# Mamba block and mixture of experts on one core: the state scan split into one-state scans, half of them with their decay in PSUM, and three rotating banks for h1 and h2

## The chip, the cores and the metric

The kernel runs on one core of a Trainium2 chip. The metric is device time in microseconds. The kernel before has a median of 1651.7 us over 3 runs (1649.79 to 1654.0).

## The reference

Input x is 32 sequences of 256 tokens with 128 features. Two layers follow, each with a residual. The first is a selective state-space block (inner width 256, 16 states); the second is a mixture of eight experts and a shared one, of which every token uses the top four by weight, all computed densely.

```python
# layer 1, on the layernorm of x
x_and_res = x @ W_in;  u, res = halves;  u = silu(u)
delta = softplus(u @ W_delta + b_delta);  Bm = u @ W_B;  Cm = u @ W_C;  A = -exp(A_log)
# for each token in order, h is (256, 16) per sequence
h = exp(delta[..., None] * A) * h + delta[..., None] * Bm[:, None, :] * u[..., None]
y_t = einsum('bdn,bn->bd', h, C_t)
x = x + ((y + u * D) * silu(res)) @ W_out
# layer 2, on the layernorm of the new x; H = 341
gate = x @ Wg.T + bias;  weights = softmax over the top 4 of 8
h1, h2 = x @ W1[e].T, x @ W2[e].T
out = shared(x) + sum_e weights[e] * ((sigmoid(h1) * h1 * h2) @ W3[e].T)
```

## The kernel before

The tokens are cut into 16 tiles of 512 (two sequences each). Every tile goes through a chain of steps, and each of the five engine programs has a written order of steps (SP_ORDER, PE_ORDER, ACT_ORDER, DVE_ORDER, POOL_ORDER). The order is one body of a software pipeline: the letter ahead of a step says which tile it works on (SHIFT: f is tile j+1, m is j, e is j-1, d is j-2, c is j-3, b is j-4). Bodies -1 to 5 are written out, 6 to 14 run in a hardware loop (Fori), 15 to 19 are written out again; a body at either end leaves out the parts whose tile doesn't exist.

The first layer of a tile. xT, wi, wi_res, dz, bt, ct are TensorE steps into the one `side` bank; ScalarE and VectorE read them (L466, L540, L541, L611). GpSimd makes `delta` and `du` (L428, L433). b_out and bbc on the SyncE queue write the B rows to memory and read them back spread over all partitions, two states (1024 elements) at a time. The 16 states are handled in 8 groups of two (GN), the 256 channels in two halves (NH), so there are 16 units (NU), `arg` = 2 x group + half. For each, GpSimd writes du x B of both states into a ring buffer `hb` (dbu, L440), ScalarE writes two exponentials into a ring of eight `decay` buffers (decay, L552), and VectorE runs one scan in place over both states, 1024 elements (scan, L617). Column 0 of each sequence of `decay` is a zero set once, which restarts the scan. TensorE then turns the states (turn.0 to 31, four 128x128 transposes each, L802) into two `turn` banks, where VectorE multiplies by C and adds up in `acc` (sum, L630); state 0 is done by ScalarE (first, L525). Then yT, z, ymul, wo and x1 end the layer.

The second layer of a tile. x1T, xh and xl split the normalized input into a high and a low part. There are 24 hidden tiles of 128: h12.k is six matmuls (L836 to L838) of which three fill an h1 bank and three an h2 bank, two banks of each. silu.k (L563) reads h1 on ScalarE, gated.k (L694) multiplies it by h2 on VectorE into a ring of eight, w3.k (36 steps, L847) multiplies by W3 into `eo_bank`, ev.0 to 8 (L701, L706) add the experts up. gate, gate_exp, gem, ginv and w compute the routing weights.

ScalarE needs one table for exponentials and another for silu; a switch in the order is a table load (L490).

PSUM has eight banks: two h1, two h2, one `eo_bank`, two `turn`, one `side`.

The waits that the change touches. h1 of tile k waits for silu k-2, and h2 of tile k for gated k-2:

```python
for banks, hi, lo, free, full in ((h1_bank, w1h, w1l, s_ready, h1_full),
                                  (h2_bank, w2h, w2l, gated_ready, h2_full)):
    wait_before(pe, free, turn, NK, arg - 1)
```

dbu waits until the transposes of the group that used its buffer are done (`turned_before`, from HB_RING), turn waits until both scans of its group are done.

Of the kernel before, what the change touches and what calls it, by code (L numbers as in the profile page):

```python
# [6 lines left out]
ALU = mybir.AluOpType  # L7
# [3 lines left out]
P = 128  # L11
SEQ = 256
# [4 lines left out]
NS = 16  # L17
# [36 lines left out]
HB_RING = 4  # L54
BB_RING = 4
GATED_RING = 8
S_RING = 3
GATE_STEPS = 12
ABSENT = -3.0e38
CHOSEN = 3.0e38  # L60
TABLE_OF = {"soft": "natural_log_exp_and_others", "decay": "natural_log_exp_and_others",
# [11 lines left out]
d:turn.11 c:w3.6.7 d:wi_res.1 d:turn.12 c:h12.10 d:turn.13.14 c:w3.8.9.10 e:xT.0 c:w3.11 c:h12.11.12 e:wi.0  # L73
d:turn.15 c:w3.12 c:h12.13 d:turn.16.17 e:wi.1 d:turn.18 c:w3.13.14 c:h12.14.15 d:turn.19 c:w3.15 e:bt.0
d:turn.20.21 c:h12.16.17 d:turn.22 e:dz.0 c:h12.18 d:turn.23 c:w3.16.17.18.19 d:turn.24 e:dz.1 c:h12.19.20
d:turn.25 c:w3.20.21 d:turn.26.27.28.29.30.31 c:w3.22 d:yT.0 c:w3.23 d:yT.1 c:h12.21 c:w3.24.25.26.27 c:h12.22
# [16 lines left out]
e:scan.5 d:gated.5.6 e:sum.7
# [20 lines left out]
def mamba_moe_kernel(nc, x, w_in, w_delta, b_delta, w_b, w_c, a_log, d_param, w_out, wg_t, bias, w1_all,  # L114
# [7 lines left out]
    SHIFT = {"f": 1, "m": 0, "e": -1, "d": -2, "c": -3, "b": -4}  # L122
# [25 lines left out]
    with ctx:  # L148
# [40 lines left out]
        decay = sb("decay", [P, DA_RING, GN, TOK])  # L189
# [34 lines left out]
        h1_bank = [bank(f"h1_{i}") for i in range(2)]  # L224
        h2_bank = [bank(f"h2_{i}") for i in range(2)]
# [5 lines left out]
        consts, blank = sem("consts"), sem("blank")  # L231
# [14 lines left out]
        dbu_ready, decay_ready, scanned = sem("dbu_ready"), sem("decay_ready"), sem("scanned")  # L246
# [138 lines left out]
        def _(pool):  # L385
# [8 lines left out]
            pool.memset(decay[:, :, :, :].rearrange("p r n (b t) -> p (r n b) t", t=SEQ)[:, :, 0:1], 0.0).then_inc(consts, 1)  # L394
# [67 lines left out]
        def _(act):  # L462
# [17 lines left out]
            def program(j, parts):  # L480
# [3 lines left out]
                for part, step, arg in steps["act"]:  # L484
# [18 lines left out]
                    elif step == "xh":  # L503

                        wait_before(act, h2_full, turn, NK, 0)
# [24 lines left out]
                    elif step == "bt":  # L530
                        wait_before(act, b_stored, turn, 16, 0)
                        wait_before(act, c_ready, turn, 1, 0)
                        read_side(j, parts, part, step, arg, cbT[:, :], side[0:2 * NS, :], ACT.Copy, cbT_ready)
                    elif step == "zb":

                        wait_before(act, delta_ready, turn, 1, 0)
                        wait_before(act, du_ready, turn, 1, 0)
                        wait_before(act, decay_ready, turn, NS * NH, 0)
                        act.wait_ge(side_full, side_index(j, parts, part, "dz", arg))
                        act.activation(soft[:, arg, :], side[:, :], ACT.Abs, bias=bd_sb[:, arg:arg + 1]).then_inc(soft_steps, 1)  # L540
                        act.activation(delta[:, arg, :], side[:, :], ACT.Relu, bias=bd_sb[:, arg:arg + 1]).then_inc(zb_ready, 1)  # L541
                    elif step == "soft":
                        act.wait_ge(soft_steps, count(turn, 4, 2))
                        act.activation(soft[:, :, :], soft[:, :, :], ACT.Exp, scale=-1.0).then_inc(soft_steps, 1)
                        act.wait_ge(soft_steps, count(turn, 4, 3))
                        act.activation(soft[:, :, :], soft[:, :, :], ACT.Ln, bias=one[:, :]).then_inc(soft_steps, 1)
                    elif step == "decay":
                        grp, h = divmod(arg, NH)
                        act.wait_ge(delta_ready, count(turn, 1, 1))
                        wait_before(act, scanned, turn, NU, arg - DA_RING + 1)  # L550
                        for i in range(GN):
                            act.activation(  # L552
                                decay[:, arg % DA_RING, i, :].rearrange("p (b t) -> p b t", t=SEQ)[:, :, 1:],
                                delta[:, h, :].rearrange("p (b t) -> p b t", t=SEQ)[:, :, 1:],
                                ACT.Exp, scale=a_sb[:, h, GN * grp + i:GN * grp + i + 1]).then_inc(decay_ready, 1)
                    elif step == "gate_exp":
                        act.wait_ge(gate_steps, count(turn, GATE_STEPS, GATE_STEPS))
                        wait_before(act, gem_ready, turn, 1, 0)
                        act.activation(gm[:, :, :], gm[:, :, :], ACT.Exp).then_inc(gex_ready, 1)
                    elif step == "silu":  # L560
                        act.wait_ge(h1_full, count(turn, NK, arg + 1))
                        wait_before(act, gated_ready, turn, NK, arg - S_RING + 1)
                        act.activation(s[:, arg % S_RING, :], h1_bank[arg % 2][:, :], ACT.Silu).then_inc(s_ready, 1)  # L563
                    if isinstance(j, int) and j + SHIFT[part] == 0 and (step, arg) in (("zb", 1), ("decay", 9)):
                        cut_hi(step == "decay")
# [9 lines left out]
            act.wait_ge(consts, CONSTS)  # L575
            act.wait_ge(a_ready, 1)
# [4 lines left out]
        def _(dve):  # L581
# [17 lines left out]
            def program(j, parts):  # L599
                for part, step, arg in steps["dve"]:  # L600
# [12 lines left out]
                    elif step == "scan":  # L613
                        dve.wait_ge(decay_ready, count(turn, NS * NH, GN * (arg + 1)))
# [73 lines left out]
                    elif step == "gated":  # L688
# [5 lines left out]
                        dve.tensor_tensor(gated[:, arg % GATED_RING, :], h2_bank[arg % 2][:, :],  # L694
# [13 lines left out]
                    if isinstance(j, int) and j + SHIFT[part] == 0 and (step, arg) in (("c", 0), ("scan", 9)):  # L708
                        cut_lo(step == "scan")

            dve.wait_ge(a_exped, 1)
# [6 lines left out]
        def _(pe):  # L718
# [26 lines left out]
            def program(j, parts):  # L745
                for part, step, arg in steps["pe"]:
# [43 lines left out]
                    elif step == "turn":  # L790
                        n, pair = divmod(arg, 2)
                        grp, i_n = divmod(n, GN)
                        pe.wait_ge(scanned, count(turn, NU, NH * (grp + 1)))
# [32 lines left out]
                    elif step == "h12":  # L826
# [5 lines left out]
                        for banks, hi, lo, free, full in ((h1_bank, w1h, w1l, s_ready, h1_full),  # L832
                                                          (h2_bank, w2h, w2l, gated_ready, h2_full)):
                            wait_before(pe, free, turn, NK, arg - 1)
                            dst = banks[arg % 2][:, :]
                            pe.matmul(dst, hi[:, cols], xh[:, :], start=True, stop=False)  # L836
                            pe.matmul(dst, hi[:, cols], xl[:, :], start=False, stop=False)  # L837
                            pe.matmul(dst, lo[:, cols], xh[:, :], start=False, stop=True).then_inc(full, 1)  # L838
# [63 lines left out]
```

## Time and profile before

| | before |
|---|---|
| median of 3 runs | 1651.7 us |
| the profiled execution | 1652.92 us |
| its span | 1650.2 us |
| mean granted TensorE clock | 0.969 of full speed |
| busy: TensorE, VectorE | 1482.1, 1478.1 us |
| busy: ScalarE, GpSimd | 1116.9, 953.1 us |

The span is the time between the first and the last instruction that the profiler recorded on the core. Busy time is the union of an engine's instructions. TensorE's is overstated, since matmuls overlap in the records: the distance between starts is nearer to what one costs. VectorE's instructions overlap as well, by 0.07 to 0.09 us each.

### The profile page before, as it was taken

To read this page: it belongs to the slowest core of one execution; us is meant where nothing else is said; L and a number is where in the kernel's file an instruction comes from. 1 tells how busy PE (TensorE), PEld (TensorE's weight loads), DVE (VectorE), ACT (ScalarE), POOL (GpSimd) and SP (SyncE) were. 2 spreads that over 40 slices of the span, in tenths; PEclk is the share of its full clock that TensorE was granted. 3 is DMA by queue.
4 is the path that set the end of the run, shared out by engine and by line. 5 is a ranking of instruction groups with operands and counts; after the bars stand their busy time and mean duration, and the time that the engine had idled before them with its cause. 6 is when DMAs were issued, how large, how long until landed. Compare 5 with 4: busy or idle time off the path is not lost. (4 is left out here: it accounts for less than half of the span.)

```text
span 1650.2 us, 29548 instructions
## 1 busy us (share of the span) xinstructions
PE 1482.1 (90%) x9216; PEld 1216.3 (74%) x9216; DVE 1478.1 (90%) x2755; ACT 1116.9 (68%) x1611; POOL 953.1 (58%) x477
## 2 busy tenths in 40 slices
PE   3254999999999999999999999999999999999898
PEld 0133878787887778787777878777787878878687
DVE  0797999999999999999999999999999998999943
ACT  3444787776778687676868757686876777776431
POOL 2766566575756566484656648465664747475310
PEclk9576999999999999999999999999999999999999
DMA  4211012121111112110111211012121110212000
GB/s 147 100 52 51 27 53 71 52 69 45 46 37 59 64 52 71 52 57 15 57 64 52 71 52 57 15 58 64 52 71 52 58 45 22 65 53 65 1 8 7
DMA packets 50451, 86.87 MB, mean 53 GB/s; under 512 B 4647, under 2 KB 32804, under 8 KB 50340
## 3 DMA queue, kind: packets, MB, share of 16 engines
q1 hardware_dynamic: 50340, 85.66, 15.9%
q8 instruction: 37, 0.61, 0.2%
q14 instruction: 74, 0.61, 0.1%
HBM read 80.93 MB, written 4.72 MB: 52 GB/s over the span
## 5 line engine op out<-in xcount | busy, mean ns | idle before, releaser
L440 POOL TENSOR_TENSOR hb<-du,bbc 128x1024 f32<-128x1024 f32 x256 | 721.9, 2834 | 432.4 <-PE turn L802 431.8
L617 DVE TENSOR_TENSOR_SCAN hb<-decay,hb 128x1024 f32<-128x1024 f32 x256 | 613.0, 2411 | 10.9 <-POOL hb L440 10.6
L847 PE MATMUL eo_bank<-w_sb,gated 128*128 128x128 f32 x3840 | 482.6, 276 | 2.2 <-DVE o L706 2.2
L847 PEld LDWEIGHTS eo_bank<-w_sb,gated 128*128 128x128 f32 x3840 | 459.8, 192 | 17.2 <-issue 10.3
L802 PE MATMUL turn<-ident,hb 128*128 128x128 f32 x2048 | 321.0, 285 | 112.9 <-DVE hb L617 55.2
L563 ACT ACTIVATE s<-h 128x512 f32<-128x512 f32 x384 | 224.5, 598 | 280.1 <-PE h L838 258.5
L630 DVE SCALAR_TENSOR_TENSOR acc<-turn,c_sb,acc 128x256 f32<-128x256 f32 x960 | 405.0, 475 | 8.9 <-PE turn L802 5.2
L802 PEld LDWEIGHTS turn<-ident,hb 128*128 128x128 f32 x2048 | 246.9, 146 | 218.8 <-issue 79.0
L552 ACT ACTIVATE decay<-delta,a_sb 128x510 f32<-128x510 f32 x512 | 325.5, 711 | 8.0 <-POOL delta L428 6.7
L490 ACT ACT_TABLE_LOAD x247 | 316.9, 1283 | 4.4
L694 DVE TENSOR_TENSOR gated<-h,s 128x512 f32<-128x512 f32 x384 | 258.3, 680 | 38.2 <-PE eo_bank L847 20.0
L836 PE MATMUL h<-xh,w1h 128*128 128x512 f32 x384 | 187.7, 489 | 2.0 <-DVE xl L649 2.0
L706 DVE SCALAR_TENSOR_TENSOR o<-eo_bank,w,o 128x128 f32<-128x128 f32 x512 | 143.1, 343 | 34.2 <-PE eo_bank L847 33.6
L836 PE MATMUL h<-xh,w2h 128*128 128x512 f32 x384 | 152.8, 398 | 0.0
L837 PE MATMUL h<-xl,w2h 128*128 128x512 f32 x384 | 152.4, 397 | 0.0
L838 PE MATMUL h<-xh,w1l 128*128 128x512 f32 x384 | 152.3, 397 | 0.0
L838 PE MATMUL h<-xh,w2l 128*128 128x512 f32 x384 | 151.9, 395 | 0.0
L837 PE MATMUL h<-xl,w1h 128*128 128x512 f32 x384 | 151.7, 395 | 0.0
L838 PEld LDWEIGHTS h<-xh,w2l 128*128 128x128 f32 x384 | 72.4, 189 | 18.0
L836 PEld LDWEIGHTS h<-xh,w2h 128*128 128x128 f32 x384 | 72.5, 189 | 17.3 <-DVE gated L694 0.3
L837 PEld LDWEIGHTS h<-xl,w2h 128*128 128x128 f32 x384 | 72.5, 189 | 17.3
L838 PEld LDWEIGHTS h<-xh,w1l 128*128 128x128 f32 x384 | 72.3, 188 | 17.4
(81 smaller groups left out, 1186.9 us busy)
## 6 DMA issues: line engine op xcount, KB each, us to landing
bbc<-b_rows SPq DMA_DIRECT2D x128, 512.0 KB, 4.8
x_in<-x_dram SPq DMA_DIRECT2D x16, 256.0 KB, 2.8
x_cur<-x_dram SPq DMA_DIRECT2D x16, 256.0 KB, 3.0
out_dram<-o SPq DMA_DIRECT2D x16, 256.0 KB, 2.4
gated<-w_all_dram SPq DMA_DIRECT2D x2, 1534.5 KB, 7.3
w_sb<-w_all_dram SPq DMA_DIRECT2D x5, 192.0 KB
b_rows<-cbT SPq DMA_DIRECT2D x16, 32.0 KB, 1.6
w_in_sb<-w_in_dram SPq DMA_DIRECT2D x1, 256.0 KB, 3.1
```

Of the source, the lines that this page charges most:

```text
L440: pool.tensor_tensor(hb[:, arg % HB_RING, :, :], du[:, h, :].unsqueeze(1).broadcast_to((P, GN, TOK)), bbc[:, r, :].rearrange("p (n t) -> p ...
L490: act.preload_act_table_set(table)
L552: act.activation(decay[:, arg % DA_RING, i, :].rearrange("p (b t) -> p b t", t=SEQ)[:, :, 1:], delta[:, h, :].rearrange("p (b t) -> p b t" ...
L563: act.activation(s[:, arg % S_RING, :], h1_bank[arg % 2][:, :], ACT.Silu).then_inc(s_ready, 1)
L617: dve.tensor_tensor_scan(states, decay[:, arg % DA_RING, :, :].rearrange("p n t -> p (n t)"), states, 0.0, ALU.mult, ALU.add).then_inc(sca ...
L630: dve.scalar_tensor_tensor(acc[:, blk, :], turn_bank[pair][:, i * DI:(i + 1) * DI], c_sb[:, blk, n:n + 1], acc[:, blk, :], ALU.mult, ALU.add)\
L694: dve.tensor_tensor(gated[:, arg % GATED_RING, :], h2_bank[arg % 2][:, :], s[:, arg % S_RING, :], ALU.mult).then_inc(gated_ready, 1)
L802: mm = pe.transpose(turn_bank[pair][:, (NH * i + h) * P:(NH * i + h + 1) * P], src[:, blk * P:(blk + 1) * P], ident[:, :])
L836: pe.matmul(dst, hi[:, cols], xh[:, :], start=True, stop=False)
L837: pe.matmul(dst, hi[:, cols], xl[:, :], start=False, stop=False)
L838: pe.matmul(dst, lo[:, cols], xh[:, :], start=False, stop=True).then_inc(full, 1)
L847: mm = pe.matmul(eo_bank[:, blk * P:(blk + 1) * P], gated[:, k % GATED_RING, blk * P:(blk + 1) * P], w3_sb[:, pair, :], start=(n == 0), st ...
```

## The change

- A scan of two states (1024) becomes two steps, scan0 and scan1, of one state (512) each; each has a semaphore of its own (`scanned[i]`), and turn waits only for the scans of its own state.
- The decay of the even state of a group (decay0) goes to one PSUM bank, `decay_bank`, which holds one decay. decay0 of unit k waits for scan0 of unit k-1. The odd state's decay1 stays in a ring of eight buffers in SBUF, each half the size.
- `hb` has 8 buffers instead of 4.
- h1 and h2 are steps of their own on TensorE. They take turns in three banks: h1.k fills bank 2k mod 3, h2.k bank 2k+1 mod 3. h1.k waits for gated k-2, h2.k for silu k-1.
- All five orders are new. The parts b and a do work now (a: tile j-5, the store), so the pipeline is one body longer and the hardware loop runs from body 7.

```diff
-HB_RING = 4
+HB_RING = 8
+H_RING = 3
@@
-c:load_cur.0 c:bbc.4.5.6.7 d:b_out.0 d:bbc.0.1.2.3 m:load_x.0 b:store.0
+c:bbc.4 b:load_cur.0 e:load_x.0 c:bbc.5.6.7 d:b_out.0 d:bbc.0.1.2.3 a:store.0
@@ PE_ORDER, its beginning and end
-c:w3.1 c:h12.6 c:w3.2 d:wi_res.0 c:w3.3 d:turn.8 c:h12.7 d:turn.9 c:h12.8 c:w3.4 d:turn.10 c:w3.5 c:h12.9
...
-d:wo.0 c:h12.23 e:turn.0 e:ct.0 c:w3.28 e:turn.1 c:w3.29.30.31 e:turn.2 d:x1T.0 c:w3.32.33.34.35 d:h12.0
-e:turn.3 d:h12.1 e:turn.4 d:h12.2 e:turn.5 d:h12.3 e:turn.6 d:h12.4 e:turn.7 d:gate.0 d:w3.0 d:h12.5
+c:wo.0 b:h2.7 b:h1.7 d:turn.4 b:h1.8 d:turn.5 b:w3.4.5 b:h2.8 b:w3.6 b:h2.9 b:w3.7 d:wi_res.0 b:h1.9.10 d:turn.6
...
+b:h2.21 b:h1.21.22 b:w3.24.25 e:dz.1 b:w3.26 d:turn.21.22 b:w3.27 b:h2.22.23 c:x1T.0 d:turn.23 b:h1.23
+b:w3.28.29 d:turn.24.25 b:w3.30 c:h1.0 d:turn.26 c:h2.0 b:w3.31 c:h1.1 d:turn.27 c:h2.1 d:turn.28 b:w3.32
+d:turn.29 b:w3.33 c:h2.2 c:h1.2 d:turn.30.31 c:h1.3 b:w3.34.35 d:yT.0 c:h2.3.4 c:h1.4 e:turn.0 d:yT.1 c:w3.0.1
+e:ct.0 c:w3.2 e:turn.1 c:w3.3 c:gate.0 c:h1.5 e:turn.2 c:h1.6 c:h2.5 e:turn.3 c:h2.6
@@ ACT_ORDER, all of the new one
+b:silu.16.17 d:decay0.10 d:decay1.12.13.14 d:decay0.11 e:wi.1 b:silu.18.19 d:decay0.12 b:silu.20 d:decay0.13
+e:bt.0 d:decay1.15 d:decay0.14.15 e:zb.0 b:silu.21.22 e:zb.1 e:soft.0 c:x1T.0 c:xh.0 b:silu.23 e:decay1.0
+c:silu.0.1 e:decay1.1 e:decay0.0 e:decay1.2.3 e:decay0.1 c:silu.2.3.4 e:decay0.2 m:xn.0 e:first.0 e:decay0.3
+e:first.1 c:silu.5.6 e:decay1.4.5.6 e:decay0.4 c:gate_exp.0 c:silu.7.8 e:decay0.5 e:decay1.7.8.9 e:decay0.6
+e:wi_res.0 c:silu.9.10 e:ud.0 e:wi_res.1 c:silu.11.12 e:ud.1 c:silu.13 e:decay0.7 e:decay1.10 e:decay0.8
+e:decay1.11 m:xT.0 e:decay0.9 c:silu.14.15 d:x1n.0 m:wi.0
@@ DVE_ORDER, all of the new one
+b:ev.1 d:sum.5.6 b:gated.9 d:scan0.6 b:gated.10 d:scan1.4 b:gated.11 d:scan1.5.6 d:sum.7.8 b:ev.2 b:gated.12
+d:scan0.7 d:sum.9.10 d:scan0.8 b:gated.13 d:sum.11 b:ev.3 d:sum.12 b:gated.14.15 d:scan0.9 d:scan1.7 b:gated.16
+d:scan1.8.9 d:scan0.10 d:sum.13.14 b:gated.17 d:scan0.11 d:sum.15 b:gated.18 b:ev.4 d:sum.16.17 d:scan0.12
+b:gated.19 d:scan1.10 b:gated.20 d:scan0.13 d:sum.18 b:ev.5 d:scan0.14 d:scan1.11 d:sum.19 d:scan1.12 d:sum.20
+d:scan1.13.14 b:gated.21 d:sum.21 b:ev.6 d:scan1.15 d:sum.22.23 c:xl.0 b:gated.22 d:sum.24.25 b:gated.23
+d:scan0.15 d:sum.26 b:ev.7 d:sum.27 c:gated.0 d:sum.28.29 e:scan0.0 c:gated.1 d:sum.30.31 e:scan0.1 c:gated.2
+d:z.0 b:ev.8 c:gated.3 e:scan1.0 d:z.1 e:scan1.1 e:c.0 e:scan0.2 c:gated.4 c:ev.0 c:gate.0 e:sum.2 e:scan0.3
+c:gated.5 e:scan1.2 c:gated.6 e:sum.3 f:ln.0 e:scan0.4 d:x1.0 c:gated.7 e:scan1.3 c:ginv.0 e:scan0.5 e:sum.4
+c:gated.8
@@ POOL_ORDER
-c:dbu.15 d:delta.0 d:du.0 d:dbu.0.1 c:ymul.0 d:dbu.2 c:rstd1.0 d:dbu.3.4 m:rstd.0 d:dbu.5.6 c:gem.0 d:dbu.7
-c:w.0 d:dbu.8.9.10.11.12.13.14
+b:w.0 d:dbu.7.8.9.10 c:rstd1.0 d:dbu.11.12.13.14.15 m:rstd.0 e:delta.0 e:du.0 e:dbu.0.1.2.3 d:ymul.0 e:dbu.4.5
+c:gem.0 e:dbu.6
@@ banks
-        h1_bank = [bank(f"h1_{i}") for i in range(2)]
-        h2_bank = [bank(f"h2_{i}") for i in range(2)]
+        h_bank = [bank(f"h_{i}") for i in range(H_RING)]
+        decay_bank = bank("decay_bank")
@@ ScalarE
-                    elif step == "decay":
+                    elif step in ("decay0", "decay1"):
+                        i = int(step[-1])
...
-                        wait_before(act, scanned, turn, NU, arg - DA_RING + 1)
-                        for i in range(GN):
+                        wait_before(act, scanned[i], turn, NU, arg if i == 0 else arg - DA_RING + 1)
+                        dst = decay_bank[:, :] if i == 0 else decay[:, arg % DA_RING, :]
@@ VectorE
-                        states = hb[:, arg % HB_RING, :, :].rearrange("p n t -> p (n t)")
-                        dve.tensor_tensor_scan(states,
-                                               decay[:, arg % DA_RING, :, :].rearrange("p n t -> p (n t)"),
-                                               states, 0.0, ALU.mult, ALU.add).then_inc(scanned, 1)
+                        states = hb[:, arg % HB_RING, i, :]
+                        dve.tensor_tensor_scan(states, decay_bank[:, :] if i == 0 else decay[:, arg % DA_RING, :],
+                                               states, 0.0, ALU.mult, ALU.add).then_inc(scanned[i], 1)
@@ TensorE
-                        pe.wait_ge(scanned, count(turn, NU, NH * (grp + 1)))
+                        pe.wait_ge(scanned[i_n], count(turn, NU, NH * (grp + 1)))
...
+                        if step == "h1":
+                            wait_before(pe, gated_ready, turn, NK, arg - 1)
+                            hi, lo, fill, full = w1h, w1l, 2 * arg, h1_full
+                        else:
+                            wait_before(pe, s_ready, turn, NK, arg)
+                            hi, lo, fill, full = w2h, w2l, 2 * arg + 1, h2_full
+                        dst = h_bank[fill % H_RING][:, :]
```

## Rows read from the trace of the kernel before

**Rows 1.** The page, part 1: busy us, share of span, instructions of each engine.

```profile
PE 1482.1 (90%) x9216; PEld 1216.3 (74%) x9216; DVE 1478.1 (90%) x2755; ACT 1116.9 (68%) x1611; POOL 953.1 (58%) x477
```

**Rows 2.** Busy time of each engine in stretches: start:end, length, PE, PEld, DVE, ACT, POOL.

```profile
69.32:139.34 70.02, 35.10 (x136) 22.88 (x136) 65.72 (x76) 33.19 (x44) 51.13 (x19) 0.73 0.15 54
...
274.12:367.30 93.18, 90.50 (x578) 74.92 (x577) 89.63 (x173) 69.94 (x102) 57.94 (x30) 1.00 0.18 55
1509.49:1596.53 87.04, 78.79 (x512) 68.10 (x511) 71.64 (x147) 39.96 (x59) 28.18 (x15) 0.98 0.03 10
1596.53:1650.20 53.67, 48.38 (x318) 42.94 (x316) 21.14 (x52) 11.56 (x19) 0.49 (x2) 1.00 0.02 6
```

**Rows 3.** TensorE in order of time: start, length, line, shapes, count.

```profile
806.03 0.48 PE L836 MATMUL h<-xh,w1h 128*128 128x512 f32 x1
...
807.51 2.84 PE L847 MATMUL eo_bank<-w_sb,gated 128*128 128x128 f32 x24
810.11 0.48 PE L836 MATMUL h<-xh,w1h 128*128 128x512 f32 x1
```

**Rows 4.** VectorE's waits (total, times, longest): two from 274.12:367.3, two from 842.89:938.9.

```profile
DVE gated L694 <- PE eo_bank L847: 1.1, 1, 1.1
DVE xl L649 <- ACT xh L508: 0.9, 1, 0.9
...
DVE gated L694 <- PE eo_bank L847: 1.6, 2, 0.9
...
DVE o L701 <- issue: 0.7, 1, 0.7
```

**Rows 5.** SyncE's register instructions of the looped output store: durations, first and last start.

```profile
L378 SPq FUSED_REGOPS  x9: 57/57/57, 447.8 to 1214.3; - x9
```

**Rows 6.** VectorE, GpSimd and ScalarE in order of time, one looped body.

```profile
831.87 0.69 DVE L694 TENSOR_TENSOR gated<-h,s 128x512 f32<-128x512 f32 x1
832.46 0.87 DVE L630 SCALAR_TENSOR_TENSOR acc<-turn,c_sb,acc 128x256 f32<-128x256 f32 x2
833.25 2.29 DVE L617 TENSOR_TENSOR_SCAN hb<-decay,hb 128x1024 f32<-128x1024 f32 x1
...
845.82 5.01 ACT L552 ACTIVATE decay<-delta,a_sb 128x510 f32<-128x510 f32 x8
...
848.64 7.00 POOL L440 TENSOR_TENSOR hb<-du,bbc 128x1024 f32<-128x1024 f32 x2 [4.35 <-PE turn L802]
...
849.83 3.63 DVE L617 TENSOR_TENSOR_SCAN hb<-decay,hb 128x1024 f32<-128x1024 f32 x1
...
853.96 1.11 DVE L706 SCALAR_TENSOR_TENSOR o<-eo_bank,w,o 128x128 f32<-128x128 f32 x4
...
880.61 4.46 DVE L617 TENSOR_TENSOR_SCAN hb<-decay,hb 128x1024 f32<-128x1024 f32 x2
```

**Rows 7.** One line's instructions over the run: ns min/median/max, first and last start.

```profile
L617 DVE TENSOR_TENSOR_SCAN hb<-decay,hb x256: 2258/2281/4437, 45.9 to 1554.6; 128x1024 f32<-128x1024 f32 x128
...
L694 DVE TENSOR_TENSOR gated<-h,s x384: 657/681/695, 164.7 to 1638.5; 128x512 f32<-128x512 f32 x192
```

**Rows 8.** The scans' busy time in an unrolled body and in a looped one.

```profile
274.12:367.30 93.18, 36.70 (x16) 1.00 0.18 55
...
733.20:829.30 96.10, 38.02 (x16) 1.00 0.16 53
```

**Rows 9.** The page's groups: busy, mean ns of one | idle before, releaser.

```profile
L440 POOL TENSOR_TENSOR hb<-du,bbc 128x1024 f32<-128x1024 f32 x256 | 721.9, 2834 | 432.4 <-PE turn L802 431.8
...
L490 ACT ACT_TABLE_LOAD x247 | 316.9, 1283 | 4.4
```

**Rows 10.** VectorE in order of time: at tile 0's `xl`, and after the last `acc`.

```profile
160.99 0.69 DVE L649 TENSOR_TENSOR xl<-side,xh 128x512 fp32r<-128x512 f32 x1 [4.35 <-ACT xh L508]
...
1564.31 0.68 DVE L694 TENSOR_TENSOR gated<-h,s 128x512 f32<-128x512 f32 x1
```

**Rows 11.** The page, part 6: a DMA group, KB each, us to landing.

```profile
bbc<-b_rows SPq DMA_DIRECT2D x128, 512.0 KB, 4.8
```

More of the change, by code:

```diff
@@ L60 @@
 CHOSEN = 3.0e38
-TABLE_OF = {"soft": "natural_log_exp_and_others", "decay": "natural_log_exp_and_others",
+TABLE_OF = {"soft": "natural_log_exp_and_others", "decay0": "natural_log_exp_and_others",
+            "decay1": "natural_log_exp_and_others",
             "gate_exp": "natural_log_exp_and_others", "wi": "silu_and_others", "wi_res": "silu_and_others",
@@ L188, in mamba_moe_kernel @@
         bbc = sb("bbc", [P, BB_RING, GN * TOK])
-        decay = sb("decay", [P, DA_RING, GN, TOK])
+        decay = sb("decay", [P, DA_RING, TOK])
         hb = sb("hb", [P, HB_RING, GN, TOK])
@@ L245, in mamba_moe_kernel @@
         bbc_in = [sem(f"bbc_in_{r}") for r in range(BB_RING)]
-        dbu_ready, decay_ready, scanned = sem("dbu_ready"), sem("decay_ready"), sem("scanned")
+        dbu_ready = sem("dbu_ready")
+        decay_ready = [sem(f"decay_ready_{i}") for i in range(GN)]
+        scanned = [sem(f"scanned_{i}") for i in range(GN)]
         turned, summed = sem("turned"), sem("summed")
@@ L503, in program @@
                     elif step == "xh":
+                        wait_before(act, h1_full, turn, NK, 0)
                         wait_before(act, h2_full, turn, NK, 0)
@@ L537, in program @@
                         wait_before(act, du_ready, turn, 1, 0)
-                        wait_before(act, decay_ready, turn, NS * NH, 0)
+                        for i in range(GN):
+                            wait_before(act, decay_ready[i], turn, NU, 0)
                         act.wait_ge(side_full, side_index(j, parts, part, "dz", arg))
@@ L562, in program @@
                         wait_before(act, gated_ready, turn, NK, arg - S_RING + 1)
-                        act.activation(s[:, arg % S_RING, :], h1_bank[arg % 2][:, :], ACT.Silu).then_inc(s_ready, 1)
-                    if isinstance(j, int) and j + SHIFT[part] == 0 and (step, arg) in (("zb", 1), ("decay", 9)):
-                        cut_hi(step == "decay")
+                        act.activation(s[:, arg % S_RING, :], h_bank[2 * arg % H_RING][:, :], ACT.Silu).then_inc(s_ready, 1)
+                    if isinstance(j, int) and j + SHIFT[part] == 0 and (step, arg) in (("zb", 1), ("decay1", 9)):
+                        cut_hi(step == "decay1")
             def cut_hi(second):
@@ L575, in _ @@
             act.wait_ge(consts, CONSTS)
+            act.wait_ge(bank_blank, 1)
             act.wait_ge(a_ready, 1)
@@ L707, in program @@
                                                          ALU.mult, ALU.add).then_inc(ev_done, 1)
-                    if isinstance(j, int) and j + SHIFT[part] == 0 and (step, arg) in (("c", 0), ("scan", 9)):
-                        cut_lo(step == "scan")
+                    if isinstance(j, int) and j + SHIFT[part] == 0 and (step, arg) in (("c", 0), ("scan1", 9)):
+                        cut_lo(step == "scan1")
+            dve.memset(decay_bank[:, :].rearrange("p (b t) -> p b t", t=SEQ)[:, :, 0:1], 0.0).then_inc(bank_blank, 1)
+            dve.wait_ge(bank_blank, 1)
             dve.wait_ge(a_exped, 1)
@@ L825, in program @@
                         mm.then_inc(side_full, 1)
-                    elif step == "h12":
+                    elif step in ("h1", "h2"):
                         cols = slice(arg * P, (arg + 1) * P)
@@ L831, in program @@
                                 pe.wait_ge(w_lo, 2)
[L832 to L838, printed above, removed]
+                        if step == "h1":
[5 more added lines that the diff above has]
+                        dst = h_bank[fill % H_RING][:, :]
+                        pe.matmul(dst, hi[:, cols], xh[:, :], start=True, stop=False)
+                        pe.matmul(dst, hi[:, cols], xl[:, :], start=False, stop=False)
+                        pe.matmul(dst, lo[:, cols], xh[:, :], start=False, stop=True).then_inc(full, 1)
                     elif step == "w3":
```

39 lines of the change are left out of this document (14 added, 25 removed).

## The prediction

> **What bounds the kernel now.** I read the page's busy shares first: TensorE and VectorE both show 90% of the span, ScalarE 68%, GpSimd 58% [rows 1]. Two engines at 90% leave open which one sets the pace, so the next view is the busy time by stretch, cut at the start of each body of the program (the first `o<-eo_bank` of a tile on VectorE marks it). An unrolled body lasts 93.18 us and VectorE is busy 89.63 of it; TensorE's 90.50 overstates its load, since matmul records overlap [rows 2]. By their starts, the six matmuls of one hidden tile take 1.48 us (806.03 to 807.51) and 24 of the `eo_bank` ones 2.60 (807.51 to 810.11), 0.108 each [rows 3]. So a tile's MoE costs TensorE 24 x 1.48 = 35.5 and 240 x 0.108 = 26.0, its 128 transposes at the same 0.108 another 14; with about 13 for projections and side work, an estimate, that is some 88. VectorE is the bound, full but for 3.5 us of a body, of which the view of waits names 1.1 for `eo_bank` and 0.9 for `xh` [rows 4].
>
> Bodies inside the hardware loop are longer. The output stores of the nine looped bodies run from 447.8 to 1214.3: 766.5 / 8 = 95.8 us [rows 5]. The same stretch of orders in the loop shows where 2.6 us go: VectorE restarts late (0.7, "issue"), `gated` waits 0.5 more for TensorE, and one scan takes 3.63 us instead of 2.28 [rows 4, 6]. That last is a collision: two `hb` products on GpSimd began at 848.64, the scan at 849.83; the scan waited 1.35 us for the first product and the second product for the scan, so the two took 7.00 us [rows 6]. While one engine runs, the other waits. `gated`, with one operand in PSUM, never stretches: at most 695 ns over a median of 681, against 4437 over 2281 for a scan [rows 7].
>
> **The change, part by part.**
> *Scans.* 256 scans of 1024 become 512 of 512. A scan of 1024 costs 2.19 us when another follows (two in 4.46, one in 2.28 [rows 6, 7]). If an element takes two cycles of 0.96 GHz (1024 x 2 = 2133 ns), 57 ns are fixed; no row has a scan of another size, so this is an estimate. The nearest rows bound it: `gated`, PSUM and SBUF in, starts its successor after 0.60 us, 0.067 above 512/0.96; `acc`, 256 from PSUM, two in 0.79, costs 0.39, which leaves 0.125 [rows 6]. Lowest is no added cost, highest 0.125 in each new scan: +0 to +3 us a tile over 35.0. I take 0.057, the operation's own remainder: +0.9.
> *Half the decays in PSUM.* The port conflict goes for 16 of 32 scans. What is there to win is small: the 16 scans of an unrolled body take 36.70 against 16 x 2.281 = 36.50, so 0.2 us; in a looped one 38.02, so 1.5 [rows 7, 8]. GpSimd gets back some of what it waits (its product's mean is 2.83 us), but it idles 432 us before these products [rows 9] and is not late. Gain 0.1 us unrolled, 0.6 looped. The bounds are 0 and the full 0.2 and 1.5.
> *ScalarE.* The 32 exponentials stay (0.62 us each in a row, 8 in 5.01 [rows 6]). The order has 20 switches between the exponential and the silu table instead of 16, at 1283 ns: +5.1 us on an engine busy 69.94 of 93.18 [rows 2, 9]. Hidden in sum, but the bank for `decay0` holds one decay, so ScalarE and VectorE now alternate. The tightest stretch by my reading is decay0.10 to decay0.13: after decay0.10 ScalarE does 5 more exponentials up to decay0.12 (three decay1, two decay0), wi.1, silu.18 and 19, silu.20, decay0.13 and four table loads, 6 x 0.62 + 4 x 0.6 + 4 x 1.28 = 11.2 us. VectorE in the same stretch has three scan0 and one scan1 (4 x 1.12), sum.13 to 17 (5 x 0.78), gated.17 to 20 (4 x 0.6) and ev.4 (four `o` steps, 1.11 in a row, 1.04 without the overlap with the next [rows 6]): 11.8 us. It fits with 0.6 to spare, so I charge nothing; the cost if it does not fit is a rival.
> *Three banks.* h2(k) now waits for silu(k-1) and h1(k) for gated(k-2), where both had two banks of their own. TensorE loses one hidden tile half of running ahead (0.70 us) in each of ScalarE's exponential blocks, and has w3 and turn steps between. Bound 0 to 8 x 0.7 = 5.6 of its 6 us of slack; I take 0 for the period. Twice as many `hb` buffers (8) take away much of what GpSimd waits for; of VectorE's 3.5 idle I let 0.8 go.
> So an unrolled body is 89.7 + 0.9 - 0.1 + 2.7 = 93.2, no shorter than now; the loop's excess falls from 2.6 to 2.0.
> *Queues.* In SP's order load_cur and load_x, which wait for x1 and xn, now stand ahead of bbc.5 to 7, where they stood before bbc.4 and behind bbc.3; on GpSimd delta and du stand behind dbu.15, ymul behind dbu.3 of the next tile. A `bbc` transfer lands in 4.8 us [rows 11], GpSimd has over 30 us idle in a body of 93.18 (58 busy) [rows 2], and 8 `hb` buffers let products run ahead. I charge nothing; if a late x1 holds bbc.5 up, the scans behind it stand still for the same time, at most 4.8 a body.
> *The pipeline.* This is the part that moves the end. In the old order h12.0 of a tile stands beside turn.3 of the next; in the new one h1.0 stands behind turn.26 of the next, and parts b and a are new stages. The MoE of a tile is 23 of 32 transposes later. Steady bodies do not care; filling and draining do.
> Fill: VectorE went to tile 0's MoE up to 161.0 with a wait of 4.35 for `xh` [rows 10], and shorter ones before it. In the new order tile 1 reaches sum.4 without these and without tile 0's first `gated`, at about 158, an estimate. The next body (tile 1's scans, tile 2's start, the first seven hidden tiles of tile 0) lacks 15 `gated` and 32 `o` steps, 15 x 0.6 + 8 x 1.04 = 17.3: 90.5 - 17.3 + some 6.8 idle (tile 0 alone had 4.3 idle in 70.0 [rows 2]) = 80. Full bodies begin at 238.
> Full bodies 4 to 16: 13 x 93.2 + 8 looped x 2.0 = 1227.6.
> Body 17 (last scans, no new tile): the old one took 87.04 with 78.8 TensorE busy [rows 2]; the new one has less side work, 84.
> Drain: after the last `acc` at 1564.3 the old kernel needed 85.9 us [rows 10]. The old last body (18 hidden tiles, 35 w3 steps of 6.7 matmuls or 0.72 us) is 18 x 1.48 + 35 x 0.72 = 51.8 by rows and took 53.67 [rows 2, 3], so 1.9 over. The new one has body 18: 17 hidden tiles and 32 w3 steps of tile 14, then wo, x1T and gate (28 matmuls, 3.1), seven hidden tiles and four w3 steps of tile 15: 24 x 1.48 + 36 x 0.72 + 3.1 = 64.5; and body 19 with 17 x 1.48 + 32 x 0.72 = 48.2. With 1.9 over each, 116.
> Span 238 + 1227.6 + 84 + 116 = 1665.6. The same sum for the old kernel is 180.8 + 14 x 94.9 + 87.0 + 53.7 = 1650.2 (the first is what is left: body 17 begins at 1509.5, and 14 bodies lie before it). The profiled execution took 1652.92 with that span, 2.7 more, and lies 1.2 above the median of 1651.7. So 1665.6 + 2.7 - 1.2 = **1667**.
>
> In other words: filling and draining cost 18 us more, the shorter loop excess gives 5 back, the rest about 3.
>
> **Rivals.** *VectorE's idle goes.* The finer steps and 8 `hb` buffers might close the gaps: a body of 91.5 (90.5 busy, 1.0 idle) and only the loop's 0.65 restart: 438 + 13 x 91.5 + 8 x 0.65 = 1633 span, 1634. For it: nearly all of today's idle is four named waits. Against: VectorE's load itself does not fall. The point from which this kernel beats the old one is a body of 92.0.
> *Handshake through one bank.* ScalarE reaches decay0 late, and scan0 waits, at the four tight places of a body, 0.5 us each (half a silu or a late TensorE step): +2 x 14 = 28, 1695. For: a spare of 0.6 us in 11.8, one wait on PE in it breaks it. Against: the other decay0 have 0.7 us or more. It decides from 0.6 us of delay per lap.
> *PSUM read at full fixed price.* scan0 pays 0.125 as `acc` does, not 0.057: 16 x 0.068 = 1.1 a body, +15, 1682. For: `acc` reads PSUM. Against: so does `gated`, with 0.067. The Trainium skill, "VectorE: DVE Perf Modes", section on the TRN2 errata, gives 120 fixed cycles from PSUM against 58 from SBUF; an estimate by it is 62 cycles, 65 ns, for each scan0, the same 15 us. No row here shows a scan reading PSUM.
> *No change in sum.* Body at 92.0 to 92.3, 1650 to 1655.
> *The change doesn't free the port.* Then the looped collision stays: +0.6 x 8 = 5, inside the range. [...]
>
> **Numbers.** Forecast or near it (1657 to 1676) 0.35; fixed price 0.13; handshake 0.12; VectorE's idle goes 0.27; no change 0.13. A measurement tells 0.3%, 5 us, from none. Faster than 1646.7: 0.28; within 5 us of 1651.7: 0.13; slower: 0.59. The range leaves a tenth at each end: 1632 to 1694; that of the forecast alone is 1657 to 1676.
>
> **What would show it.** Scan groups with a mean near 1.21 us, scan0 with a maximum near its median and scan1 not; 32 of them 36 us of a body. VectorE's unrolled bodies near 93, looped ones near 95. The first `gated` of tile 0 near 210 instead of 164.7, and after the last `acc` some 125 us instead of 86. ScalarE with about 20 table loads a body and no scan0 waiting for it. It would be wrong if bodies fell below 92, if scan0 waits for ScalarE, if `gated` or h waits on each other's banks for over 1 us a body, or if the drain takes under 110 us.

## The result and the profile after

The changed kernel takes 1610.4 us (median of 4 runs, 1608.65 to 1611.48), the kernel before 1652.85 in the same comparison (4 runs): a ratio of 0.974, 95% interval 0.972 to 0.976. It is 42 us faster; 15 slower had been forecast, with 1632 as the low end of the range. The profiled execution took 1608.65 with a span of 1606.9.

The stretches of VectorE's bodies, as in [rows 2]: an unrolled body (start:end, length, then busy PE, PEld, DVE, ACT, POOL), a looped one, and the drain from the last `acc` on.

```profile
308.09:397.94 89.85, 88.93 (x578) 74.77 (x578) 89.47 (x190) 74.93 (x106) 49.69 (x30) 1.00 0.16 57
761.19:852.85 91.66, 89.33 (x578) 74.78 (x578) 89.87 (x189) 74.93 (x106) 49.78 (x30) 1.00 0.16 55
1478.90:1606.90 128.00, 122.69 (x799) 108.68 (x797) 58.42 (x165) 34.53 (x57) 4.91 (x9) 1.00 0.03 9
```

The unrolled body fell from 93.18 to 89.85 us, and VectorE is busy 89.47 of it, where it was 89.63 of 93.18 [rows 2]. It has nearly the same work; its idle time went from 3.55 to 0.38 us. The looped body fell from 96.0 to 91.7 us, and there both parts shrank: busy time from 91.42 to 89.87, idle time from 4.6 to 1.8. The old kernel's looped body:

```profile
842.89:938.90 96.01, 91.38 (x573) 75.59 (x572) 91.42 (x172) 69.26 (x100) 58.42 (x30) 0.98 0.17 53
```

The page's groups after (busy, mean ns of one | idle before, releaser), against [rows 7, 9]:

```profile
L450 POOL TENSOR_TENSOR hb<-du,bbc 128x1024 f32<-128x1024 f32 x256 | 617.6, 2436 | 217.0 <-PE turn L817 212.7
...
L631 DVE TENSOR_TENSOR_SCAN hb<-decay_bank,hb 128x512 f32<-128x512 f32 x256 | 310.2, 1212 | 13.3 <-POOL hb L450 12.0
L631 DVE TENSOR_TENSOR_SCAN hb<-decay,hb 128x512 f32<-128x512 f32 x256 | 316.2, 1252 | 0.0
```

GpSimd's product costs 2436 ns instead of 2834: it hardly waits for scans. Over the run (ns min/median/max) the scans with the PSUM decay never stretch, those with two SBUF operands do, at most to 3297:

```profile
L631 DVE TENSOR_TENSOR_SCAN hb<-decay_bank,hb x256: 1190/1210/1225, 45.6 to 1470.2; 128x512 f32<-128x512 f32 x128
L631 DVE TENSOR_TENSOR_SCAN hb<-decay,hb x256: 1190/1210/3297, 49.1 to 1464.1; 128x512 f32<-128x512 f32 x128
```

VectorE has two waits in the looped body (total, times, longest); for the unrolled body the same view names none:

```profile
DVE o L719 <- issue: 1.1, 1, 1.1
DVE acc L643 <- PE turn L817: 0.2, 1, 0.2
```

The waits of [rows 4] for `eo_bank` and `xh` are gone from both bodies. "issue" is VectorE's restart after the loop's branch.

A scan with both operands in SBUF and a product of GpSimd exclude each other [rows 6]; what they contend for is called the port here. How the new orders keep clear of it shows in one stretch of a looped body, in order of time. The product pair at 795.12 runs under `acc`, `gated` and other work, the scan at 799.17 is a PSUM one, and SBUF scans follow only once the pair is done, at 799.86.

```profile
795.12 4.74 POOL L450 TENSOR_TENSOR hb<-du,bbc 128x1024 f32<-128x1024 f32 x2 [0.92 <-PE turn L817]
...
799.17 1.21 DVE L631 TENSOR_TENSOR_SCAN hb<-decay_bank,hb 128x512 f32<-128x512 f32 x1
800.30 1.20 DVE L631 TENSOR_TENSOR_SCAN hb<-decay,hb 128x512 f32<-128x512 f32 x1
```

The run split by the forecast's own terms, in us. Body 4, body 17 and the drain begin at 234.25, 1414.48 and 1497.94, each marked by the first `o<-eo_bank,w,o` of a tile:

| | forecast | measured |
|---|---|---|
| until body 4 | 238 | 234.3 |
| bodies 4 to 16 | 1227.6 | 1180.2 (90.8 each) |
| body 17 | 84 | 83.5 |
| drain | 116 | 109.0 |
| span | 1665.6 | 1606.9 |

### The profile page after: what moved, and what is told of

It reads as the page before. It is cut to its first block, busy times and chain, and to the rows that moved or that the text cites. A ratio compares the mean times of both kernels' runs of the same rounds, so it can differ in the third digit from the quotient of the medians.

```text
span 1606.9 us, 30312 instructions
## 1 busy us (share of the span) xinstructions
PE 1470.4 (92%) x9216; PEld 1215.4 (76%) x9216; DVE 1461.6 (91%) x3012; ACT 1176.7 (73%) x1659; POOL 805.8 (50%) x477
## 4 chain that ended last, share of the span: by engine, by line
PE 64%; DVE 13%; issue 10%; ACT 9%; POOL 3%; DMA 1%; DVEq 1%; SPq 0%; ACTq 0%; POOLq 0%
PE eo_bank L865 20%; PE turn L817 9%; PE h L854 9%; PE h L855 8%; PE h L856 8%; DVE hb L631 6%; PE side L787 3%; PE side L781 3%; DVE acc L643 2%; ACT L500 2%; PE side L794 2%; POOL hb L450 2%; DVE gated L707 2%; ACT decay L565 1%; DVE o L719 1%
## 5 line engine op out<-in xcount | busy, mean ns | idle before, releaser
L450 POOL TENSOR_TENSOR hb<-du,bbc 128x1024 f32<-128x1024 f32 x256 | 617.6, 2436 | 217.0 <-PE turn L817 212.7
L865 PEld LDWEIGHTS eo_bank<-w_sb,gated 128*128 128x128 f32 x3840 | 472.2, 192 | 40.2 <-issue 18.0
L865 PE MATMUL eo_bank<-w_sb,gated 128*128 128x128 f32 x3840 | 495.5, 276 | 7.2 <-DVE o L719 7.2
L631 DVE TENSOR_TENSOR_SCAN hb<-decay_bank,hb 128x512 f32<-128x512 f32 x256 | 310.2, 1212 | 13.3 <-POOL hb L450 12.0
L631 DVE TENSOR_TENSOR_SCAN hb<-decay,hb 128x512 f32<-128x512 f32 x256 | 316.2, 1252 | 0.0
L565 ACT ACTIVATE decay_bank<-delta,a_sb 128x510 f32<-128x510 f32 x256 | 175.6, 686 | 153.2 <-DVE hb L631 152.0
L707 DVE TENSOR_TENSOR gated<-h,s 128x512 f32<-128x512 f32 x384 | 257.5, 674 | 30.6 <-PE h L856 14.1
L854 PE MATMUL h<-xh,w2h 128*128 128x512 f32 x384 | 180.7, 471 | 0.7 <-ACT s L575 0.7
L565 ACT ACTIVATE decay<-delta,a_sb 128x510 f32<-128x510 f32 x256 | 170.6, 708 | 7.0 <-POOL delta L438 6.5
L438 POOL TENSOR_TENSOR delta<-delta,soft 128x1024 f32<-128x1024 f32 x16 | 37.9, 2368 | 231.6 <-ACT soft L558 231.6
L456 POOL TENSOR_TENSOR y<-y,sres 128x1024 f32<-128x1024 f32 x16 | 50.5, 3159 | 108.9 <-DVE y L649 108.9
```

What stands on the lines that cost most here:

```text
L450: pool.tensor_tensor(hb[:, arg % HB_RING, :, :], du[:, h, :].unsqueeze(1).broadcast_to((P, GN, TOK)), bbc[:, r, :].rearrange("p (n t) -> p ...
L565: act.activation(dst.rearrange("p (b t) -> p b t", t=SEQ)[:, :, 1:], delta[:, h, :].rearrange("p (b t) -> p b t", t=SEQ)[:, :, 1:], ACT.Ex ...
L631: dve.tensor_tensor_scan(states, decay_bank[:, :] if i == 0 else decay[:, arg % DA_RING, :], states, 0.0, ALU.mult, ALU.add).then_inc(scan ...
L707: dve.tensor_tensor(gated[:, arg % GATED_RING, :], h_bank[(2 * arg + 1) % H_RING][:, :], s[:, arg % S_RING, :], ALU.mult).then_inc(gated_r ...
L865: mm = pe.matmul(eo_bank[:, blk * P:(blk + 1) * P], gated[:, k % GATED_RING, blk * P:(blk + 1) * P], w3_sb[:, pair, :], start=(n == 0), st ...
```

## The experiments

Each was timed in 4 runs beside the kernel before; the medians of that kernel were 1651.8 (e1 to e4), 1653.0 (e5 to e8) and 1652.2 (e9 to e11).

### e1: decay0 in SBUF

```diff
-        decay_bank = bank("decay_bank")
+        decay_bank = sb("decay_bank", [P, TOK], mybir.dt.bfloat16)
```

> The changed kernel with decay0's one buffer in SBUF instead of PSUM (as bf16, since SBUF has no room for 2 KB; so the decays of the even states are rounded). The orders, the three banks and the eight hb buffers stay. Theory P (the port): the changed kernel lost VectorE's idle because 16 of 32 scans of a tile no longer take the second SBUF port. Then scan0 collides again with the hb products of GpSimd: its maximum goes from 1225 ns to over 2000, the products' mean from 2436 to 2700 or more, and a body grows by 2 to 4 us, 1640 to 1665. Theory S (slack): the idle went because the new orders and eight hb buffers let every engine run ahead, and the port is worth only what scans were seen to lose before (0.2 us an unrolled body, 1.5 a looped one). Then collisions come back but a body grows by under 1 us, 1611 to 1625.

1746.9 us, ratio 1.058 (1.056 to 1.060), 136 above the changed kernel. The scans and products of this kernel:

```profile
L450 POOL TENSOR_TENSOR hb<-du,bbc 128x1024 f32<-128x1024 f32 x256 | 687.0, 2705 | 229.5 <-PE turn L817 222.9
L631 DVE TENSOR_TENSOR_SCAN hb<-decay_bank,hb 128x512 f32<-128x512 bf16 x256 | 443.3, 1732 | 13.3 <-POOL hb L450 12.2
```

```profile
L631 DVE TENSOR_TENSOR_SCAN hb<-decay_bank,hb x256: 1191/1226/3422, 47.8 to 1605.1; 128x512 f32<-128x512 bf16 x128
```

The minimum is that of the PSUM scans (1190), so neither the type nor the place makes a scan longer by itself; the mean went from 1212 to 1732. 443.3 - 310.2 = 133 us more in scan0 and 6 in scan1 make up the whole difference of the spans (1741.8 - 1606.9 = 135). An unrolled body of this kernel:

```profile
259.63:357.50 97.87, 90.40 (x576) 74.81 (x576) 97.51 (x189) 75.34 (x106) 56.28 (x30) 1.00 0.16 52
```

VectorE is busy 97.51 of 97.87 us: it idles 0.36, no more than in the changed kernel (0.38), and is busy 8.1 us longer. So theory P is right that the port decides, at 136 us instead of the 30 to 55 it gave, but wrong on the idle time. VectorE's waits are gone with the port conflict back as well; what the PSUM decay saves in these orders is stretched scans.

### e2: the old kernel with split scans

```diff
-                        states = hb[:, arg % HB_RING, :, :].rearrange("p n t -> p (n t)")
-                        dve.tensor_tensor_scan(states,
-                                               decay[:, arg % DA_RING, :, :].rearrange("p n t -> p (n t)"),
-                                               states, 0.0, ALU.mult, ALU.add).then_inc(scanned, 1)
+                        for i in range(GN):
+                            states = hb[:, arg % HB_RING, i, :]
+                            scan = dve.tensor_tensor_scan(states, decay[:, arg % DA_RING, i, :], states, 0.0,
+                                                          ALU.mult, ALU.add)
+                        scan.then_inc(scanned, 1)
```

> The kernel before with each scan of 1024 as two scans of 512, back to back, all in SBUF, nothing else changed. By the prediction a split adds 57 ns: 16 x 0.057 = 0.9 us a body, +14 over 15 bodies, 1666. The rival: the changed kernel's body shows VectorE busy 89.47 us where the old one shows 89.63, so a split costs VectorE less than 10 ns: 1650 to 1656. If a fixed price as acc's were paid it would be 1680.

1728.6 us, ratio 1.046 (1.044 to 1.048): 77 slower, outside all three expectations. The scans' mean is 1457 ns at a minimum of 1189, 721 us in all against 613. Two places in order of time, VectorE without and with a product of GpSimd that starts beside it:

```profile
862.75 2.33 DVE L618 TENSOR_TENSOR_SCAN hb<-decay,hb 128x512 f32<-128x512 f32 x2
...
895.35 4.45 DVE L618 TENSOR_TENSOR_SCAN hb<-decay,hb 128x512 f32<-128x512 f32 x2
```

```profile
895.46 6.53 POOL L440 TENSOR_TENSOR hb<-du,bbc 128x1024 f32<-128x1024 f32 x2 [4.91 <-PE turn L803]
```

The pair alone takes 2.33 us where one scan took 2.28, so a split costs 0.05, near the 0.057 forecast. But a scan of 1024 held the port through, as in [rows 6], where the second product waited for it; between two halves the waiting product takes it, and the second half stands for it (2.1 us more). The split by itself is a loss. Whether it would pay in the old order with one half's decay in PSUM was not tried.

### e3: the old kernel with three banks

```diff
-        h1_bank = [bank(f"h1_{i}") for i in range(2)]
-        h2_bank = [bank(f"h2_{i}") for i in range(2)]
+        h_bank = [bank(f"h_{i}") for i in range(3)]
...
-                        for banks, hi, lo, free, full in ((h1_bank, w1h, w1l, s_ready, h1_full),
-                                                          (h2_bank, w2h, w2l, gated_ready, h2_full)):
-                            wait_before(pe, free, turn, NK, arg - 1)
-                            dst = banks[arg % 2][:, :]
+                        for fill, hi, lo, free, back, full in ((2 * arg, w1h, w1l, gated_ready, 1, h1_full),
+                                                               (2 * arg + 1, w2h, w2l, s_ready, 0, h2_full)):
+                            wait_before(pe, free, turn, NK, arg - back)
+                            dst = h_bank[fill % 3][:, :]
...
```

> The kernel before with h1 and h2 in three rotating banks under the new waits (h1.k for gated k-2, h2.k for silu k-1), in the old order, pairs as they were. It prices the lost bank by itself. By the prediction 0 up to 5.6 us a body: TensorE has 5 us of slack, so 1650 to 1660 if w3 and turn steps cover it. The rival: in an order not made for it TensorE stands while ScalarE is in its exponential blocks (up to 7.6 us with two table loads), and VectorE waits behind: 2 to 5 us a body, 1680 to 1720. That would say that the separate h1 and h2 steps are what makes three banks free.

1758.3 us, ratio 1.063 (1.061 to 1.066): +107. TensorE's and VectorE's longest waits over the run (total, times, longest):

```profile
PE h L836 <- ACT s L563: 78.7, 66, 3.4
```

```profile
DVE acc L630 <- PE turn L802: 86.9, 66, 3.3
```

TensorE stands for silu and the transposes behind it come late; `acc` waited 5.2 us for them in the old kernel. Three banks are not free in an order that wasn't made for them.

### e4: the changed kernel unrolled

```diff
-            for j in range(FIRST, LOOP[0]):
+            for j in range(FIRST, LAST + 1):
                 program(j, body_parts(j))
-            with eng.Fori(*LOOP) as j:
-                program(j, ALL)
-            for j in range(LOOP[1], LAST + 1):
-                program(j, body_parts(j))
```

> The changed kernel with all bodies written out and no hardware loop. Unrolled bodies last 89.85 us, looped ones 91.6. If that excess is the restart of each engine after the branch, 8 bodies x 1.75 = 14 us go: 1596. The rival: it is the fetching of code that was not there, then a program without a loop fetches more of it and gains nothing or loses: 1605 to 1625.

1596.4 us, ratio 0.966 (0.964 to 0.968), 14.0 less than the changed kernel, as computed from the loop's excess (what a looped body takes more than an unrolled one). This is the fastest version of all.

### e5: h1 and h2 side by side again

```diff
+    pe = steps["pe"]
+    for k in range(NK):
+        part, = {p for p, s, a in pe if s in ("h1", "h2") and a == k}
+        at = max(pe.index((part, "h1", k)), pe.index((part, "h2", k)))
+        pe[at:at + 1] = [("", "both", k)]
+        pe = [step for step in pe if step not in ((part, "h1", k), (part, "h2", k))]
+        at = pe.index(("", "both", k))
+        pe[at:at + 1] = [(part, "h1", k), (part, "h2", k)]
+    steps["pe"] = pe
```

> The changed kernel with h1.k and h2.k put next to each other in TensorE's order, both at the place of the later one; all else as changed. It asks whether h1 and h2 as steps of their own carry the three banks. Theory L (leave to run ahead): the old order with three banks lost 106 us, since pairs make TensorE wait for silu with both halves; then this loses too, 2 to 6 us a body, 1640 to 1700. The rival: the old order lost only because its silus stood in the wrong places, and the changed orders of ScalarE and VectorE fit three banks either way: 1608 to 1620.

1741.4 us, ratio 1.052 (1.050 to 1.054): +131, above the range of theory L. Two of VectorE's waits over the run (one for `xh`, 36.6 us, lies close behind), and an unrolled body:

```profile
DVE hb L640 <- ACT decay_bank L574: 42.6, 34, 1.7
DVE gated L716 <- PE h L865: 39.4, 47, 2.0
```

```profile
337.31:436.04 98.73, 90.83 (x579) 75.23 (x577) 91.96 (x189) 75.32 (x106) 50.23 (x30) 1.00 0.16 52
```

The first row is the handshake that the prediction named as a rival: scan0 waits for ScalarE's decay0. That it does so because h, and with it silu, is late is read from the order of steps. In the changed kernel that wait came once, for 1.2 us. In the body VectorE idles 6.8 us where the changed kernel idles 0.38, so the separate h1 and h2 steps are what keeps its waits away here.

### e6 and e7: eight hb buffers in the old order, and its control

The edit of e6 is the following; e7 changes DA_RING alone.

```diff
-DA_RING = 8
-HB_RING = 4
+DA_RING = 4
+HB_RING = 8
```

> The kernel before with eight hb buffers; to make room its decay ring has four units instead of eight. Theory B (buffers): VectorE's 3.5 idle us a body and the loop's collision come from GpSimd's products, held back by the hb ring (it idles 432 us for turns). With eight buffers in the old order the body falls to 91 to 92 and the run to 1625 to 1640. Theory O (orders): the order text, not the ring, fixes where products fall, and eight buffers alone only let GpSimd start at other moments, so collisions with scans rise or stay: 1650 to 1690.

> The control of the run above: the kernel before with the decay ring at four units and four hb buffers. Where the decay ring matters, ScalarE's blocks of eight exponentials (units 0 to 4 in a row) wait for scans: 1655 to 1680. Where not, 1650 to 1655, and the run above is read against the kernel before.

e7 1734.1 us (ratio 1.048, 1.045 to 1.051), e6 1813.5 (1.095, 1.093 to 1.098). The shorter decay ring cost 81, more than expected: ScalarE's decays wait 162.5 us for scans, and `gated` waits 24.4 us for silu instead of 1.8. On top of that eight buffers cost 79 more: GpSimd idles 52.8 us for `turn` instead of 506.5, starts earlier, and the scans' mean rises. The two rows are e7's and e6's scans:

```profile
L617 DVE TENSOR_TENSOR_SCAN hb<-decay,hb 128x1024 f32<-128x1024 f32 x256 | 628.2, 2471 | 12.6 <-POOL hb L440 12.4
```

```profile
L617 DVE TENSOR_TENSOR_SCAN hb<-decay,hb 128x1024 f32<-128x1024 f32 x256 | 693.2, 2724 | 12.7 <-POOL hb L440 12.5
```

65 of the 79 us are that. Of the two theories O holds: eight buffers alone are harm in the old order, where every scan takes the port. It is shown with the short decay ring only.

### e8: the old kernel unrolled

The edit is that of e4.

> The kernel before with all bodies written out. The changed kernel won 14 us by that. Old looped bodies last 96.1 us against 93.24 unrolled, so 9 x 2.8 = 25 us go if the excess (restart of VectorE 0.7, later TensorE 0.5, collided scan 1.35) is all due to the branch: 1627. If the collision is there without the branch too: 1640. It also says how much of the change's 42 us is only that it suffers less from the loop: compared unrolled with unrolled, 1627 to 1596 would leave 31.

1629.7 us, ratio 0.985 (0.984 to 0.987): 23.3 less of the 25 expected. The scans' mean fell from 2411 to 2369 ns, so the collided scan of [rows 6] went with the loop. Unrolled against unrolled the change is worth 33.3 us; the other 9 of its 42 are that it suffers less from the loop (14.0 against 23.3), in which it also runs one body fewer (8 against 9).

### e9: half of the decay0 in SBUF

```diff
+        decay_odd = sb("decay_odd", [P, TOK], mybir.dt.bfloat16)
...
-                        dst = decay_bank[:, :] if i == 0 else decay[:, arg % DA_RING, :]
+                        dst = (decay_odd if arg % 2 else decay_bank)[:, :] if i == 0 else decay[:, arg % DA_RING, :]
...
```

The scan reads the same buffer.

> The changed kernel with decay0 in PSUM for the first half of the channels (even units) and in an SBUF buffer (bf16) for the second (odd units), waits as changed. It is the dose between the changed kernel (1610) and decay0 all in SBUF (1747). If each collided scan0 costs what it is stretched by, VectorE being full, half the scans bring about half: 60 to 80 us, 1670 to 1690, the PSUM scans' maximum stays at 1225 ns and the SBUF ones' mean is near 1732. If it were the handover between ScalarE and VectorE through one buffer, two buffers would relax it: under 1640.

1724.3 us, ratio 1.044 (1.042 to 1.046): 114 more than the changed kernel, not 60 to 80. The scans by operand:

```profile
L632 DVE TENSOR_TENSOR_SCAN hb<-decay_odd,hb 128x512 f32<-128x512 bf16 x128 | 240.7, 1880 | 1.2 <-POOL hb L451 1.1
...
L632 DVE TENSOR_TENSOR_SCAN hb<-decay_bank,hb 128x512 f32<-128x512 f32 x128 | 154.9, 1210 | 11.8 <-POOL hb L451 10.6
```

In kind it confirms the port: PSUM scans stay at 1210 ns, with a maximum of 1224, beside stretched SBUF ones, and a second buffer relaxed nothing. The size isn't linear: the odd ones are stretched by 670 ns each, where e1's are by 520 on average. That is 86 us; scan1 adds 9.5 (1289 against 1252 ns), and VectorE's waits for h, 27.3 us against 14.1, another 13. Half of the SBUF scans cost five sixths of what all of them do. Why the odd units are stretched more was not traced.

### e10 and e11: half the tiles

```diff
-    NT = x.shape[0] * x.shape[1] // TOK
+    NT = x.shape[0] * x.shape[1] // TOK // 2
```

> The changed kernel, all bodies written out, with 8 of the 16 tiles; the other half of the output is not computed. Time = fill and drain + tiles x body. With a body of 89.85 and 1596.4 for 16 tiles it takes 877.6; 8 tiles cost 718.8. The other reading, that the deeper pipeline is not the cost but the last bodies run differently, would show as another slope.

> The kernel before, all bodies written out, with 8 of the 16 tiles; the other half of the output is not computed. With a body of 93.24 and 1629.7 for 16 tiles it takes 883.8. The two intercepts (time at 8 tiles less 8 bodies) are then 158.8 for the changed kernel and 137.9 for the old, 21 apart: by the prediction the pipeline's lag costs 18. If filling and draining cost nothing more, both intercepts are equal and the changed kernel takes 857 at 8 tiles.

878.6 us for the changed kernel, 884.8 for the old one, both unrolled. Slopes: (1596.4 - 878.6) / 8 = 89.7 and (1629.7 - 884.8) / 8 = 93.1 us a tile. Intercepts: 878.6 - 8 x 89.7 = 161 and 884.8 - 8 x 93.1 = 140. Filling and draining cost the changed kernel 21 us more, its body saves 3.4: by these lines the two would be even at 6 tiles, and at 16 it wins 33.

## Why the prediction was wrong, step by step

**The failed step: "of VectorE's 3.5 idle I let 0.8 go".** All but 0.4 went. The forecast's bodies 4 to 16 were 47 us too long, 80% of the span's miss of 59. By the trace VectorE idles 16 us in these 13 bodies, and the forecast gave 35 for idle time and 16 for the loop; that is 35 of the 47, and the other 12 are its busy time, 89.6 us a body instead of 90.5. I had the right bound and the right reading that its idle was a few named waits, and then kept the waits. The rival "VectorE's idle goes" was the right mechanism, held at 0.27; it was also priced too dear (a body of 91.5, 1634).

What the runs show in its place: with h1 and h2 put side by side again the idle is back, 6.8 us a body (e5), so the separate steps are needed to be rid of it. The port is not what removed it: with the conflict back it stays at 0.36 (e1). Whether the other new orders, the later MoE or the eight `hb` buffers are needed too stays open.

**The step under it: "what is there to win is small".** Against the old kernel that was nearly so: in an unrolled body VectorE's busy time fell by 0.2 us, in a looped one by 1.5, where 0.6 had been put down for the port. But it is the price with an order arranged around the conflict, not the worth of being free of it. e1 puts the port conflict back into the new orders and loses 136 us, 8.1 in an unrolled body. The old side shows the same: GpSimd idled 432 us for `hb` buffers [rows 9], and where it has them it starts earlier and meets more scans (e6). Its idle looked like slack; it was also cover.

**Splitting the scans: right as a term.** The split costs 0.05 us against the forecast's 0.057; the rows it names give 4.46 - 2.28 = 2.18, not 2.19, so 0.05 was in them. But VectorE's busy time didn't rise by 0.9; it fell by 0.2. `gated` (674 against 680 ns) and `acc` (471 against 475) read a little shorter: 24 x 0.006 + 60 x 0.004 = 0.4 of it. Why, and the rest of the gap, was not traced.

**The fixed price of a PSUM read is refuted.** Both kinds of scan have a median of 1210 ns. The Trainium skill's page "VectorE: DVE Perf Modes", section on the TRN2 errata, has 62 cycles between its SBUF and its PSUM column. They would be 65 ns, an estimate by that page, and do not show for a scan; the measurement decides.

**ScalarE: right.** The profile's page counts 295 table loads, about 20 a body; decay0 waits for scan0 (152 us in all), and scan0 waited for decay0 once, 1.2 us.

**Three banks: right for this order, wrong as a general price.** h waited 0.7 us for `gated` in the unrolled body and 1.2 in the looped one, a little over the 1 us that the prediction had named as a sign of being wrong. The bound, 5.6 us a body, was too low for other orders: 107 and 131 us in e3 and e5 are 7 to 9 in each of some 15 bodies.

**Loop: the excess fell to 1.8 us a body, forecast 2.0.** The restart of VectorE stays (1.1 against 0.7), the collision is gone.

**The pipeline: right in size.** 18 us had been forecast; the intercepts of e10 and e11 say 21. Body 4 began at 234.3 (238), the last `acc` lay 128.0 us before the end ("some 125"), the first `gated` came at 204.9 ("near 210"). The drain was forecast 7 us too long, and at 109.0 it is below the 110 that the prediction had named as a sign of being wrong. Some 3 of the 7 are that I took 1.48 us for each of 41 hidden tiles, and the six matmuls cost 1.40 where they follow one another; the rest was not traced.

**The port rival** ("the change doesn't free the port") is refuted by 1225 ns as the maximum of 256 scans.

What stays open: what else it takes, besides the separate h1 and h2 steps, to bring the idle from 3.55 to 0.38 us. e1 and e5 show that this order can't do without the PSUM decay and the separate steps (136 and 131 us); e6 shows that eight buffers are no gain in the old order. That the waits for `eo_bank` and `xh` went because the MoE lags is argued from their absence, not shown. The new orders with four `hb` buffers can't be run: dbu.10 would wait for turn.15, turn.15 for sum.13, sum.13 stands behind scan0.10, and scan0.10 waits for dbu.10.

## What to carry to other kernels

When the bounding engine's load stays the same, ask what its remaining idle is made of and whether the change allows those few waits to be reordered away; here four named waits (1.1, 0.9, 0.8 and 0.2 us in an unrolled body) made up 3.0 of 3.5 us. Price a shared resource by what the schedule does to keep clear of it, not by the collisions left in the trace: the idle time of another engine may be what keeps the two apart. In a schedule this tight, no part of a change can be priced alone: the three pieces tried in the old order cost 77 us (split scans), 107 (three banks) and 79 (eight buffers, over a control with the short decay ring), and together with new orders and the PSUM decay they gain 42.

## What the runs showed of the hardware

- A scan of 512 takes 1210 ns and its successor starts after 1.12 us; one of 1024 takes 2281. The difference, 1071 ns for 512 elements, is 2.09 ns an element.
- A scan with two SBUF operands kept GpSimd's product waiting until it ended (two products took 7.00 us around one scan of 1024 [rows 6]). Cut in two, GpSimd got in between, and the second part waited for most of a product (up to 3361 ns for a scan with a median of 1208, e2). With one operand in PSUM 256 scans stayed at or below 1225 ns beside the same products.
- An exponential written to PSUM takes 690 ns (median), to SBUF 707.
- The hardware loop cost this program 1.8 us an iteration in the new kernel (14.0 over 8) and 2.6 in the old one (23.3 over 9). Of a price for the longer code little shows: in e4, VectorE has two waits of 0.3 us between 600 and 1000 us that no engine explains.
